# Second edge list in groups of one tile, a sum per tile, and edge weights read from PSUM

## The reference, cut to what matters

```
m_e      = W_forward xn[src] * d_e0 + W_reverse xn[src] * d_e1      (64 features)
score_eh = leaky_relu(attn_h . m_e, 0.2)                            (4 heads)
p_eh     = exp(score_eh - max) / sum over the edges of dst of exp(score - max)
x[dst]  += sum over edges and heads of p_eh * m_e
```

## Time and profile before

| | |
|---|---|
| median of 3 runs | 2914.25 us (2913.68 to 2917.84) |
| profiled execution, its own time | 2912.84 us |
| its span | 2910.9 us |
| busy in the span: PE, DVE, ACT, POOL | 74%, 57%, 41%, 70% |
| first and last gather of the second edge list | 1814.9 us, 2405.3 us |

### The profile page before, as it was taken

The page is one execution under the profiler, slowest core; times in us unless marked ns, Lnnn a source line. Parts: engine busy times, 40 slices in busy tenths (PEclk is TensorE's granted clock), DMA queues, the critical chain, the costliest instruction groups (busy, mean ns, idle before and its releaser), DMA issues. The chain is left out here.

```text
span 2910.9 us, 34578 instructions
## 1 busy us (share of the span) xinstructions
PE 2167.6 (74%) x10021; PEld 1675.2 (58%) x10021; DVE 1673.6 (57%) x4649; ACT 1187.8 (41%) x3164; POOL 2037.0 (70%) x2064
## 2 busy tenths in 40 slices
PE   0275482277766768999999997688877776999994
PEld 0054361144444447878888876455555455888883
DVE  8937899366679885111000125788887766333236
ACT  0111354155555542222222213699954444344443
POOL 4777777677777776777777633777777773777761
PEclk9996555588888887999999999899987876999997
DMA  2020000533333341356666632322222241111111
GB/s 65 2 63 2 6 3 2 191 105 105 105 104 103 102 98 35 121 163 200 195 197 198 191 105 91 95 53 54 53 52 52 52 49 11 29 32 36 17 19 47
DMA packets 173391, 233.36 MB, mean 80 GB/s; under 512 B 59819, under 2 KB 136622, under 8 KB 172206
## 3 DMA queue, kind: packets, MB, share of 16 engines
q0 software_dynamic: 73664, 103.00, 15.6%
q1 hardware_dynamic: 96504, 117.82, 13.1%
q10 hardware_dynamic: 3062, 10.68, 1.0%
HBM read 192.31 MB, written 39.04 MB: 79 GB/s over the span
## 5 line engine op out<-in xcount | busy, mean ns | idle before, releaser
L831 POOL DMA_INDIRECT slots_gnn<-rec_gnn,slot_row_gnn x782 | 771.3, 986 | 286.4 <-issue 229.9
L2408 POOL DMA_INDIRECT arena<-table,rec_gnn x440 | 457.5, 1040 | 161.9 <-issue 124.7
L1222 POOL DMA_INDIRECT rows_gnn<-support,xT x416 | 401.2, 964 | 132.7 <-issue 110.9
L1266 PE MATMUL banks<-rows_gnn,one_hot 128*128 128x256 f32 x832 | 304.3, 483 | 199.9 <-DMA rows_gnn<-support,xT 174.9
L1266 PEld LDWEIGHTS banks<-rows_gnn,one_hot 128*128 128x128 f32 x832 | 163.1, 228 | 322.8 <-DMA rows_gnn<-support,xT 183.8
L2986 POOL DMA_INDIRECT source_rows<-table_g,source_router x256 | 245.7, 960 | 78.0 <-issue 63.1
L2507 PE MATMUL banks<-weighted,one_hot 128*128 128x260 f32 x880 | 268.7, 458 | 3.0 <-DVE weighted L2604 2.0
L1871 ACT ACTIVATE hidden_private<-banks,b_private 128x256 f32<-128x256 f32 x256 | 107.3, 470 | 354.3 <-PE banks L1829 354.3
L1829 PE MATMUL banks<-slot_xT,w_private 128*128 128x256 f32 x1024 | 228.2, 381 | 1.7 <-DVE slot_xT L1885 1.7
L1841 PE MATMUL banks<-w_private,hidden_private 128*128 128x256 f32 x1024 | 226.1, 379 | 0.0
L2507 PEld LDWEIGHTS banks<-weighted,one_hot 128*128 128x128 f32 x880 | 188.2, 224 | 61.0 <-issue 27.0
(11 more groups left out here) (576 smaller groups left out, 3976.0 us busy)
## 6 DMA issues: line engine op xcount, KB each, us to landing
w_private<-in_w1p SPq DMA_DIRECT2D x32, 1024.0 KB
w_private<-in_w2p SPq DMA_DIRECT2D x32, 1024.0 KB, 7.6
slots_gnn<-rec_gnn,slot_row_gnn POOLq DMA_INDIRECT x782, 2.1
slot_x<-zero_rows ACTq DMA_DIRECT2D x8, 1024.0 KB, 11.2
slot_rows<-slot_x SPq DMA_DIRECT2D x32, 256.0 KB, 7.0
slot_y<-slot_out SPq DMA_DIRECT2D x32, 256.0 KB, 2.2
arena<-table,rec_gnn POOLq DMA_INDIRECT x440, 2.6
rows_gnn<-support,xT POOLq DMA_INDIRECT x416, 2.7
```

Of the source, the lines that this page charges most:

```text
L831: pool.indirect_dma_start(e.slots, bass.IndirectOffsetOnAxis(e.rows[:, j:j + 1], 0), e.rec[:, j, :], None)\
L1222: pool.indirect_dma_start(e.rows_in[:, k, :], None, table, bass.IndirectOffsetOnAxis(row, 0))\
L1266: mm = pe.matmul(bank_of(k // per), hot[:, k, :], e.rows_in[:, row, :], start=k % per == 0, stop=k % per == per - 1)
L2408: pool.indirect_dma_start(c.raw[:, t % RAW_RING, :], None, c.table1, bass.IndirectOffsetOnAxis(row, 0))\
```

## The change

The second edge list is built with groups of 128, so that every tile of edges belongs to one target tile and the list is padded to 416 tiles, 52 rounds. Each tile's product is written to a bank of its own (bank k mod 4) with `start` and `stop`, and VectorE adds each tile's bank into `agg`, eight adds a round. TensorE waits for the add that frees its bank (semaphore `added`). The registers with target tiles are loaded once a round. The adds of half 0 stand right after the rescale, and not at the end of the round; scaling of v stands ahead of the adds of half 1. In `shift` the two copies stand ahead of the subtraction. ScalarE writes the exponentials twice: of the 8 tiles' weights into PSUM bank 4, and in place as before. VectorE's product reads the weights from PSUM. The ring has 64 tiles. The output of the second attention is made for two row tiles a round. In the attend stage GpSimd waits for a meeting of the other engines ahead of the table's gathers.

```diff
-RAW_RING = 72
+RAW_RING = 64
...
-        elif T + 4 <= i < 2 * T + 4:
-            t = i - T - 4
-            dve.wait_ge(self.y_ready, t + 1)
+        elif i >= T + 4:
+            for t in range(2 * (i - T - 4), min(2 * (i - T - 3), T)):
+                dve.wait_ge(self.y_ready, t + 1)
...
         def exps(i):
             act.wait_ge(shifted, i + 1)
+            act.activation(weight_room, prob[:, i % 2, 0:RING, :], ACT.Exp).then_inc(exped_there, 1)
+            act.wait_ge(exped_there, i + 1)
             act.activation(prob[:, i % 2, :, :], prob[:, i % 2, :, :], ACT.Exp).then_inc(exped, 1)
...
             for k in range(HALF * h, HALF * h + HALF):
-                mm = pe.matmul(c.bank[:, k // per, 0:AGG], hot[:, k, :], val[:, k, :, :].rearrange("p h f -> p (h f)"),
-                               start=k % per == 0, stop=k % per == per - 1)
+                n = i * RING + k
+                if n >= HALF:
+                    pe.wait_ge(added, n - HALF + 1)
+                mm = pe.matmul(c.bank[:, k % HALF, 0:AGG], hot[:, k, :], val[:, k, :, :].rearrange("p h f -> p (h f)"),
+                               start=True, stop=True)
...
             p = prob[:, i % 2, :, :]
+            mark(dve.tensor_copy(prob[:, (i + 1) % 2, RING, :], spread_room))
+            copied = mark(dve.tensor_copy(tops[:, :, i], spread_room))
+            dve.wait_ge(step, copied)
             dve.tensor_tensor(p, p, c.bank[:, 4:5, P:P + HEADS1].to_broadcast([P, RING + 1, HEADS1]), ALU.subtract)\
                 .then_inc(shifted, 1)
-            mark(dve.tensor_copy(prob[:, (i + 1) % 2, RING, :], spread_room))
-            return mark(dve.tensor_copy(tops[:, :, i], spread_room))
...
-            dve.wait_ge(exped, i + 1)
+            dve.wait_ge(exped_there, i + 1)
...
-            w = prob[:, i % 2, at:at + BY_DVE[h], :].rearrange("p t (h o) -> p t h o", o=1).to_broadcast(shape)
+            w = weight_room[:, at:at + BY_DVE[h], :].rearrange("p t (h o) -> p t h o", o=1).to_broadcast(shape)
...
         def add_half(i, h):
             dve.wait_ge(used, 2 * i + h + 1)
-            for k in range(half_groups):
-                g = half_groups * h + k
-                dve.wait_ge(step, ch.n)
-                mark(dve.tensor_tensor(tile_of(i, g), c.bank[:, g, 0:AGG], tile_of(i, g), ALU.add))
+            for g in range(HALF * h, HALF * h + HALF):
+                if i or g:
+                    dve.wait_ge(added, i * RING + g)
+                if g == 0:
+                    dve.wait_ge(step, ch.n)
+                dve.tensor_tensor(tile_of(i, g), c.bank[:, g % HALF, 0:AGG], tile_of(i, g), ALU.add).then_inc(added, 1)
...
             weigh(i, 0)
+            if 2 <= i <= T + 1:
+                mix.scale_v(dve, i - 2)
             if i:
                 add_half(i - 1, 1)
+            load_tiles(i)
             if more:
                 scaled = forward(i + 1)
-            if 2 <= i <= T + 1:
-                mix.scale_v(dve, i - 2)
-            if i % TURN == 0:
-                load_tiles(i)
...
             rescale(i)
+            add_half(i, 0)
...
-            add_half(i, 0)
             if more:
                 shift(i + 1)
...
-        pool.wait_ge(c.table_stored, 16 * c.table_stores)
+        pool.wait_ge(met, 4 * (met_n - 1))
...
-        e1 = Edges(c, "gnn1", EDGES, a["dst"], a["src"], a["edge_attr_2"], top, rounds=True)
+        e1 = Edges(c, "gnn1", EDGES, a["dst"], a["src"], a["edge_attr_2"], top, group=P, rounds=True)
```

More of the change, by code:

```diff
@@ L39 @@
 PARTS_IN_FLIGHT = FLIGHT // HALF
-BODY_GROUPS = RING * P // GROUP
+ROOM_WORDS = 1736
 NEG = -1.0e30
@@ L185, in hold_records @@
         if then_slots:
-            self.room = c.sb(ctx, f"rec_{self.name}", [P, max(self.per, self.tiles) * self.width])
+            self.room = c.sb(ctx, f"rec_{self.name}", [P, max(self.per * self.width, self.tiles * self.width, ROOM_WORDS)])
             self.rec = self.room[:, 0:self.per * self.width].rearrange("p (j w) -> p j w", w=self.width)
@@ L1185, in _ @@
           .then_inc(e.slot_in, 16)
-TURN = 3
 def tiles_of_groups(c, engine, e, first, n):
@@ L2306, in late_dve @@
                .then_inc(self.mat2_out, 1)
-        elif T + 4 <= i < 2 * T + 4:
-            t = i - T - 4
-            dve.wait_ge(self.y_ready, t + 1)
-            x = c.X[:, t, :]
-            dve.tensor_tensor(x, x, self.raw[:, t % 2, 0:D], ALU.add).then_inc(self.y_out, 1)
+        elif i >= T + 4:
+            for t in range(2 * (i - T - 4), min(2 * (i - T - 3), T)):
+                dve.wait_ge(self.y_ready, t + 1)
+                x = c.X[:, t, :]
+                dve.tensor_tensor(x, x, self.raw[:, t % 2, 0:D], ALU.add).then_inc(self.y_out, 1)
     def late_pe(self, pe, i):
@@ L2327, in late_pe @@
             mm.then_inc(self.mat2_ready, 1)
[L2328 to L2337, removed]
+        elif i >= T + 3:
+            for t in range(2 * (i - T - 3), min(2 * (i - T - 2), T)):
+                if t == 0:
+                    pe.wait_ge(self.mat2_out, 1)
+                if t >= 2:
+                    pe.wait_ge(self.y_out, t - 1)
+                out = self.raw[:, t % 2, 0:D]
+                for k in range(KD):
+                    pe.matmul(out, self.c.xT[:, k, t * P:(t + 1) * P], self.mat2[:, k, :], start=k == 0, stop=False)
+                pe.matmul(out, self.c.ones[0:1, 0:P], self.bo[:], start=False, stop=True).then_inc(self.y_ready, 1)
 class TableWeights:
@@ L2422, in sum1_stage @@
     steps = e.tiles // RING
-    assert steps >= 2 * T + 4
+    assert steps >= T + 4 + (T + 1) // 2
     tops = c.sb(ctx, "round_tops", [P, HEADS1, steps])
@@ L2439, in sum1_stage @@
     met = c.met
-    per = GROUP // P
-    half_groups = HALF // per
+    added = c.sem(ctx, "tiles_added1")
     ring_rounds = RAW_RING // RING
@@ L2447, in sum1_stage @@
     slots = lambda i: slice(i % ring_rounds * RING, i % ring_rounds * RING + RING)
+    weight_room = c.bank[:, 4, 2 * P:2 * P + RING * HEADS1].rearrange("p (t h) -> p t h", h=HEADS1)
+    exped_there = c.sem(ctx, "edge_weights_in_psum")
     @block.scalar
@@ L2602, in weigh @@
             m = c.raw[:, first:first + BY_DVE[h], 0:FEAT + 1].rearrange("p t (o f) -> p t o f", o=1).to_broadcast(shape)
-            w = prob[:, i % 2, at:at + BY_DVE[h], :].rearrange("p t (h o) -> p t h o", o=1).to_broadcast(shape)
+            w = weight_room[:, at:at + BY_DVE[h], :].rearrange("p t (h o) -> p t h o", o=1).to_broadcast(shape)
             dve.tensor_tensor(val[:, at:at + BY_DVE[h], :, :], m, w, ALU.mult).then_inc(val_dve, 1)
         def tile_of(i, g):
-            at = i * BODY_GROUPS + g
+            at = i * RING + g
             return c.agg[:, ds(tiles[at], 1), :].rearrange("p a d -> p (a d)")
@@ L2613, in rescale @@
             dve.wait_ge(step, ch.n)
+            dve.wait_ge(exped, i + 1)
+            if i:
+                dve.wait_ge(added, i * RING)
             mark(dve.tensor_tensor(x, x, f, ALU.mult))
@@ L2617, in add_half @@
             dve.wait_ge(used, 2 * i + h + 1)
-            for k in range(half_groups):
-                g = half_groups * h + k
-                dve.wait_ge(step, ch.n)
-                mark(dve.tensor_tensor(tile_of(i, g), c.bank[:, g, 0:AGG], tile_of(i, g), ALU.add))
+            for g in range(HALF * h, HALF * h + HALF):
[4 more added lines that the diff above has]
+                dve.tensor_tensor(tile_of(i, g), c.bank[:, g % HALF, 0:AGG], tile_of(i, g), ALU.add).then_inc(added, 1)
         def load_tiles(i):
-            n = min(TURN, steps - i) * BODY_GROUPS
-            first = i * BODY_GROUPS
+            first = i * RING
             tiles.clear()
-            for k, tile in enumerate(tiles_of_groups(c, mybir.EngineType.DVE, e, first, n)):
+            for k, tile in enumerate(tiles_of_groups(c, mybir.EngineType.DVE, e, first, RING)):
                 tiles[first + k] = tile
```

## The result

The changed kernel takes 3018.95 us (median of 4 runs, 3015.74 to 3024.59) against 2913.99 in the same session: ratio 1.0356, 95% interval 1.034 to 1.0371, so 105 us longer. Forecast were 2976, range 2930 to 3025.

A forecast was written before the change was run, and what follows sets the result against it. GpSimd's gathers bound the loop's second part; in the first, VectorE's chain was as long. Longer rounds gave 618 to 679 us against 587.5, 32 to 93 longer; 2912.84 + 62 + 1.4 = 2976, range 2930 to 3025.

The forecast's parts named there:

- Four more adds: VectorE's chain in the second edge list's loop: four more adds into agg cost 2.26 us per round, 1.13 in each half.
- The place of half 0's adds: Adds ahead of the variances: maximum's end to variances' end grows from 1.89 to 4.02 us; TensorE idles some 3 us.
- The product's place in PSUM: VectorE's product reading weights from PSUM: taken as 0, with ends of 6 us less to 2 more in all.
- the table load ahead of the logarithm: On ScalarE, between variances and logarithm: the table load does not wait for the variances, so it adds nothing.
- the middle of the forecast: Whole loop: midway between 32 and 93 us longer, 62 us, giving 2976; the middle case had chance 0.50.
- From the product to the score maximum: VectorE's first half of a round: 5.61 us grows to 6.91 in the first part, 5.01 to 6.3 in the second.
- The load: Register load on VectorE, behind the last add, once a round: 0.17 us per round, bounds 0 and 0.60.
- From the maximum to the product: VectorE's second half of a round: 6.0 us in the first part, 4.6 in the second.
- The wait for the spread maximum: On VectorE in the first part: some 0.3 us a round, as the adds that hid it are gone.
- The low clock: TensorE's four tiles of half 1 after idling: 1.0 us more per round in the first part, 1.5 in the second.
- it always falls: Rival: TensorE's clock is low in every round, 3007 us; chance 0.18 together with new waits on top.
- a later TensorE idles less and so keeps its clock: Reason for taking the middle, 62 us: TensorE, being later, idles less and keeps its clock for part of the rounds.

The follow-up runs named there:

- e4: The changed kernel with the adds of every second tile left out, four a round instead of eight: 2875.41 us.
- e2: The changed kernel with the adds of half 0 moved late, behind the variances, the maximum and the mix output: 2934.09 us.
- e1: The kernel before with weights in PSUM, a second exponential and the shift's copies first: 2903.53 us, ratio 0.9957.
- e5: The changed kernel with weights read from SBUF and one exponential, on another, unsteady chip: 4315.0 us, ratio 1.0162 to the kernel before.
- e9: The changed kernel with weights from SBUF and one exponential, repeated on another chip: 4350.34 us, ratio 1.0156 to the kernel before.
- e3: The changed kernel with two extra 128x512 products on TensorE in most rounds, while it waits for the diagonal: 2983.22 us.

## Why the prediction was right, and where it was too small

The mechanism was right in each step but for one reason, told last. The gathers were no longer the bound and waited 89 us for the sums. Four more adds cost 2.26 us a round on the chain of each round: e4 shows 1.13 for two of them where no wait mixes in. The place of half 0's adds, ahead of the variances, is what lets TensorE idle: 3.45 us in the round shown, as the 3 us foreseen, and e2 takes the wait away. The product's place in PSUM costs nothing, as e1 and the rounds of e5 and e9 show, and the table load ahead of the logarithm did not wait (it ran from 1999.09 to 2000.37, the logarithm's input came at 2001.1). The ring of 64 tiles and the second row tile of mix output were not tried alone; what they cost is not shown.

The size was short by 43 of 105 us. Against the middle of the forecast the rounds of the first part were 0.42 us longer (10.5 us in all) and those of the second 1.25 (30 us); what lies outside the rounds makes up the rest. By term:

- From the product to the score maximum at full clock: 7.09 us (in e3 and in the quickest rounds), foreseen 6.91. The load costs 0.31, not 0.17.
- From the maximum to the product: 6.16 at the median against 6.0, and 4.79 against 4.6. The wait for the spread maximum, foreseen as 0.3, is 0.35 in 8 rounds of the first part and 0.15 in most of the others, but 0.67 in the rounds that no longer have mix output; I had set nothing for those.
- The low clock. I took the middle between never and always. VectorE's wait for the half in the first part was the full 1.33 us in 8 of 25 rounds, nothing in 4 and something between in 13, in which the half took 2.5 to 3.7 us: 0.74 on average, where the middle was 0.5. In the second part it was 1.56 on average and 1.94 at most, where the middle was 0.75. The price at low clock was 1.33 to 1.43 us a round in the first part and up to 1.9 in the second, where I had 1.0 and 1.5: the half takes 3.83 us, not 3.65.

With these the sum is 24 + 25 times 14.09 + 24 times 13.00 = 688, against 587.5. The term that was mis-sized most is TensorE's clock, with some 25 of the 43 us (0.24 in 25 rounds, 0.81 in 24); the rest is VectorE's own way through a round. Measured is more than the case "it always falls" (3007), which had a chance of 0.18 with others, although the clock did not always fall. That 3019 lies in the range owes something to luck: the range ends at 3025, above every sum that I had worked out.

A reason that I gave for the middle was wrong: that a later TensorE idles less and so keeps its clock. The idle time lies between the turned maximum and the diagonal, while VectorE does the rescale, four adds and the variances. From round 2 on TensorE waited there 152.0 us in 49 rounds, 3.1 on average; before it was 42.4 in 51, 0.8 on average. What idle time it had before in the second part lay ahead of the transpose as well (2.5 us in the round of the earlier trace rows).

## What to carry to other kernels

Faster or fewer gathers give nothing in a stretch in which another engine's chain is as long (e1 left the first part at 11.03 us a round); look for the length of that chain round by round, not for its busy share. When work has to be added to the engine that feeds the others, put it where they have work too: with the same eight adds a round the kernel is 105 us slower than before with half 0's in one place and 19 in the other. And two SBUF inputs on VectorE slow GpSimd's gathers, so an operand that can as well lie in PSUM is worth moving where the gathers are the bound.

## What the runs showed of the hardware that I had not expected

A gather is held by VectorE at one point, some 0.13 us after its start, as the kernel before and e1 show when each gather is set against VectorE's rows. If an instruction with two SBUF inputs that began ahead of the gather is still running by then, the gather is longer by just what is left of it (0.28 us left, 1.23 instead of 0.94). An instruction that begins later does not hold it: of 53 such gathers in the kernel before none was over 0.01 us longer. And two useless products of 0.94 us in 46 of the 52 rounds made the changed kernel 36 us faster (e3).
